# Starting one score tile in seven on ScalarE in layers 1 and 2 of a three-layer graph attention kernel

## The chip, the cores and the metric

The kernel runs on one core of a Trainium2 chip. The metric is the device time in microseconds (us), lower is better. A core has TensorE (PE, matrix products into PSUM), VectorE (DVE), ScalarE (ACT, activations), GpSimd (POOL) and SyncE (SP, here the queue that starts most DMAs). They run side by side, each works through its own instructions in order, and they wait for one another on semaphores.

## The reference

Three graph attention layers over the same 8192 x 8192 adjacency matrix, 64 features a node. Layer 0 is a layer with its own weights, layers 1 and 2 are the two steps of a second block:

```python
# layer 0
scores = (Wh @ a1)[:, None] + (We @ a2)[None, :]
e = jnp.where(scores > 0, scores, ALPHA * scores)      # ALPHA = 0.2
e = jnp.where(adj > 0, e, NEG_BIG)
attention = jax.nn.softmax(e, axis=1)
x = _layernorm(x + elu(attention @ entity_embs + item_embs))
# layers 1 and 2 (i = 0, 1)
Wh = h @ W_l
e = leaky_relu(u + v.T + c)                            # u, v: one number a node
att = softmax(where(adj_mask, e, NEG_INF), axis=1)
h = ALPHA * x + (1.0 - ALPHA) * elu(att @ Wh)
# at the end
x = _layernorm(x + concat(x, h1, h2) @ mlp_w + mlp_b)
```

So each layer needs, for each pair of a row i and a neighbour j, exp of a leaky ReLU of u_i + v_j, masked by the adjacency, then its product with the features of j and the sum over j as denominator.

## The kernel before

**Tiling.** The scores are held transposed: a tile has 128 neighbours j on the partitions and 512 rows i in the free dimension. A layer has 16 blocks of 512 rows (`NB`, index b), a block has 64 tiles (`NT`, index j or t). Tile j of a block is made in four stages on three engines:

1. *The fill* puts the unmasked score into one of five PSUM buffers (`ES = 5`, `eps`). It has two forms. On DVE (`start_scores`, L1044): max(ua + v8, cb), where ua is a row made once a block (u times 0.8 plus cb), v8 one number a partition and cb the row of negated row maxima. On ACT (`start_scores`, L530): Relu(0.8 u + v8) without cb. Both can only begin when the exponential of the tile that had the buffer is done, in general tile j - 5 (`freed`).
2. *The mask product* on PE (`mask_scores`, L680) adds -9e15 where there is no edge. Where the fill was ACT's, a product ahead of it (L677) of a matrix of ones with `mrow`, the row maxima in three bf16 parts, adds cb to all partitions.
3. *The exponential* on ACT (`probs`, L538) goes from PSUM to one of eight buffers in SBUF (`prob`).
4. *The sums* on PE, once in four tiles and one group of four behind (`LAGQ = 1`): features times probabilities (L717, `acc`) and the denominators (L726, `den`).

Which tiles ACT fills is given by `ACT_TILES`, a tuple of residues of j modulo 7 for each layer, and `ON_ACT`, the set made from it for j from 3 on. Before, layer 0 has the residues 2 and 5 (17 tiles a block), layers 1 and 2 none.

**Order of the work.** It is written out by hand: at step t of a block PE does the mask product of tile t and, after every fourth, the sums of the group before; DVE fills tile t; ACT does the exponential of tile t - 1 and, where tile t + 3 (`AHEAD = 3`) is in `ON_ACT`, its fill. The end of block b - 1 (its tail: evacuate, normalise, ELU, next layer's products) and the preparation of block b + 1 (its head) are spread over the steps of block b:

- steps 35 to 43: PE counts edges by level (L690) on bytes that DVE has made (L892, steps 29 to 41); ACT copies the counts out at step 45 (L582), PE turns them at step 47 (L699);
- steps 51, 52 and 53 (`T_HEAD`): DVE does behind its fill of the step nine small instructions on the row maxima (L910 to L923), then two (L930, L931), then three (L934 to L936) that split them in bf16 parts;
- step 56: PE turns the parts (L753), ACT copies them to `mrow` (L586); step 57: PE spreads them (L758), ACT copies them to `cb` (L590); step 63: DVE makes `ua` (L1050).

The last block of a layer has no head. In layer 0 DVE also makes the bit mask from the adjacency as it arrives (L883); layers 1 and 2 read the finished mask back from HBM. At the start of a layer PE also sums the features (L704) between the tiles of block 0.

The lines that use `ON_ACT` outside the counting of semaphores:

```python
# DVE, step t
if t not in ON_ACT[l]:
    start_scores(l, b, t, par)                         # L1044
# ACT, step t, behind the exponential of tile t - 1
if t + AHEAD in ON_ACT[l]:
    start_scores(l, b, t + AHEAD, par)                 # L530
# PE, mask_scores
if on_act:
    nc.tensor.matmul(et, onesb[:, :], mrow[:, par, :], start=False, stop=False, skip_group_check=True)   # L677
```

Of the kernel before, what the change touches and what calls it, by code (L numbers as in the profile page):

```python
# [48 lines left out]
AHEAD = 3  # L49
LAGQ = 1  # L50

ACT_TILES = ((2, 5), (), ())
ON_ACT = tuple(frozenset(j for j in range(AHEAD, NT) if j % 7 in ks) for ks in ACT_TILES)
WC = 2 * C + 2

# [1124 lines left out]
```

## Time and profile before

| | |
|---|---|
| median of 3 runs | 3828.65 us (3826.26 to 3828.78) |
| the profiled execution, its own time | 3827.47 us |
| its span, first to last instruction | 3825.7 us |
| mean granted TensorE clock | 0.983 |
| PE busy (matmuls) | 3542.9 us, 93% |
| DVE busy | 2898.3 us, 76% |
| ACT busy | 2247.2 us, 59% |
| ACT fills (L530) | 272, 189.6 us |
| exponentials (L538) | 3072, 1927.5 us |

In a timeline row the columns are start (us from the span's start), time covered, engine, line, operation, output and inputs by the program's names, shapes and number of instructions, and in brackets the idle time of the engine ahead of it with what ended it. Matmuls are pipelined: each shows its whole passage, which is longer than the pitch at which they follow each other, so the distance between starts tells what one costs. Layer 1 has its first mask product at 1441.84, layer 2 at 2645.20.

### The profile page before, as it was taken

To read this page: it belongs to the slowest core of one execution; us is meant where nothing else is said; L and a number is where in the kernel's file an instruction comes from. 1 tells how busy PE (TensorE), PEld (TensorE's weight loads), DVE (VectorE), ACT (ScalarE), POOL (GpSimd) and SP (SyncE) were. 2 spreads that over 40 slices of the span, in tenths; PEclk is the share of its full clock that TensorE was granted. 3 is DMA by queue.
4 is the path that set the end of the run, shared out by engine and by line. 5 is a ranking of instruction groups with operands and counts; after the bars stand their busy time and mean duration, and the time that the engine had idled before them with its cause. 6 is when DMAs were issued, how large, how long until landed. Compare 5 with 4: busy or idle time off the path is not lost. (4 is left out here: it accounts for less than half of the span.)

```text
span 3825.7 us, 54496 instructions
## 1 busy us (share of the span) xinstructions
PE 3542.9 (93%) x21133; PEld 1136.5 (30%) x21133; DVE 2898.3 (76%) x5279; ACT 2247.2 (59%) x3947; POOL 116.3 (3%) x138
## 2 busy tenths in 40 slices
PE   1689999999999979999999999997999999999998
PEld 0323233323232324332332232323323323323322
DVE  4578888888888656777777777775777877877876
ACT  0356667667766744655655665663556556556555
POOL 0000000000000000000000000000000000000000
PEclk9999999999999988999999999997999999999999
DMA  8999999999999511122121121111111111111110
GB/s 258 292 350 338 327 337 333 336 335 332 337 338 333 170 56 51 53 81 72 59 80 65 67 77 67 67 56 67 60 66 65 72 69 65 67 73 65 64 43 6
DMA packets 414101, 578.47 MB, mean 151 GB/s; under 512 B 294402, under 2 KB 315010, under 8 KB 389266
## 3 DMA queue, kind: packets, MB, share of 16 engines
q1 hardware_dynamic: 409458, 564.40, 45.8%
q0 software_dynamic: 4384, 10.59, 0.9%
q8 instruction: 166, 2.72, 0.3%
q14 instruction: 93, 0.76, 0.1%
HBM read 430.10 MB, written 77.69 MB: 133 GB/s over the span
## 5 line engine op out<-in xcount | busy, mean ns | idle before, releaser
L538 ACT ACTIVATE prob<-eps,v2col 128x512 f32<-128x512 f32 x3072 | 1927.5, 689 | 1125.1 <-PE eps L680 1121.8
L1044 DVE SCALAR_TENSOR_TENSOR eps<-ua,v8col,cb 128x512 f32<-128x512 f32 x2800 | 1990.6, 754 | 619.2 <-ACT prob L538 609.6
L717 PE MATMUL acc<-prob,feat 128*64 128x512 f32 x6144 | 1497.8, 608 | 0.0
L680 PE MATMUL eps<-nt,nbig 128*128 128x512 fp8e4 x3072 | 903.6, 384 | 95.1 <-DVE eps L1044 95.0
L726 PE MATMUL den<-prob,ones 128*32 128x512 f32 x6144 | 820.0, 606 | 0.0
L717 PEld LDWEIGHTS acc<-prob,feat 128*64 128x64 f32 x6144 | 375.2, 136 | 744.8 <-issue 501.9
L680 PEld LDWEIGHTS eps<-nt,nbig 128*128 128x128 bf16 x3072 | 277.9, 101 | 780.9 <-DVE eps L1044 520.3
L883 DVE TENSOR_SCALAR mi<-stage 128x1024 uint8<-128x1024 int32 x512 | 351.8, 689 | 62.1 <-DMA stage<-in_adj_dram 61.9
L726 PEld LDWEIGHTS den<-prob,ones 128*32 128x32 f32 x6144 | 121.0, 108 | 626.6 <-issue 626.6
L892 DVE TENSOR_SCALAR edges<-nt 128x2048 int32<-128x2048 int32 x192 | 234.4, 1221 | 47.3 <-PE misc L690 32.5
L690 PE MATMUL misc<-edges,oneh 128*32 128x512 fp8e4 x3072 | 191.1, 391 | 71.7 <-DVE edges L892 56.9
L530 ACT ACTIVATE eps<-ub,v8col 128x512 f32<-128x512 f32 x272 | 189.6, 697 | 0.0
L690 PEld LDWEIGHTS misc<-edges,oneh 128*32 128x32 bf16 x3072 | 90.3, 99 | 192.2 <-issue 75.6
L586 ACT ACTIVATE mrow<-misc 3x512 bf16<-3x512 bf16 x48 | 28.2, 587 | 141.6 <-PE misc L753 141.6
L677 PE MATMUL eps<-mrow,onesb 128*128 128x512 bf16 x272 | 104.0, 382 | 0.0
L582 ACT ACTIVATE hs<-misc 128x512 f32<-128x512 f32 x48 | 28.3, 590 | 95.2 <-PE misc L690 95.2
L784 PE MATMUL misc<-wcat,ht 65*128 65x130 f32 x384 | 71.6, 311 | 8.6 <-ACT pj L573 6.6
L766 PE MATMUL misc<-halves,acc_s 128*128 128x64 f32 x384 | 75.8, 279 | 2.4 <-ACT hs L547 2.4
L784 PEld LDWEIGHTS misc<-wcat,ht 65*128 65x128 f32 x384 | 52.5, 198 | 69.9 <-issue 37.7
L704 PEld LDWEIGHTS misc<-feat,ones 128*128 128x128 f32 x384 | 65.8, 237 | 13.5 <-issue 10.3
L959 DVE SCALAR_TENSOR_TENSOR g<-fsum,emp,misc 128x65 f32<-128x65 f32 x192 | 41.2, 277 | 36.5 <-PE misc L768 30.2
L910 DVE TENSOR_SCALAR he<-misc 128x128 int32<-128x128 int32 x48 | 14.0, 292 | 70.9 <-PE misc L699 70.9
(140 smaller groups left out, 1251.6 us busy)
## 6 DMA issues: line engine op xcount, KB each, us to landing
stage<-in_adj_dram SPq DMA_DIRECT2D x512, 512.0 KB, 6.3
nt<-nt_d SPq DMA_DIRECT2D x128, 1024.0 KB, 5.0
nt_d<-nt SPq DMA_DIRECT2D x64, 1024.0 KB, 7.1
ub<-u_d SPq DMA_DIRECT2D x48, 256.0 KB, 5.5
xy_d<-xin POOLq DMA_DIRECT2D x32, 256.0 KB, 2.8
xin<-xy_d SPq DMA_DIRECT2D x32, 256.0 KB, 2.9
nt<-mi SPq DMA_TRANSPOSE x256, 6.7
xin<-in_x_dram SPq DMA_DIRECT2D x16, 128.0 KB, 6.1
```

Source lines behind the costliest of these rows:

```text
L530: nc.scalar.activation(eps[:, j % ES, :], ub[:, par, :], ACT.Relu, bias=v8col[:, j:j + 1], scale=1.0 - ALPHA).then_inc(s_filla, 1)
L538: nc.scalar.activation(prob[:, j % TS, :], eps[:, j % ES, :], ACT.Exp, bias=v2col[:, j:j + 1]).then_inc(s_p, 1)
L677: nc.tensor.matmul(et, onesb[:, :], mrow[:, par, :], start=False, stop=False, skip_group_check=True)
L680: nc.tensor.matmul(et, nbig[:, :], half_block(nt[:, par, m, :], m, o), start=False, stop=True, skip_group_check=True).then_inc(s_z, 1)
L690: mm = nc.tensor.matmul(misc[s * HB:(s + 1) * HB, :], oneh[:, m * MT + j, :], half_block(edges[:, n % 2, :], m, j), start=(m == 0 and k == 0),
L717: mm = nc.tensor.matmul(acc[h:h + C, :], feat[:, l % 2, j, 0:C], prob[:, j % TS, :], start=(k == 0), stop=(k == NT // 2 - 1))
L726: mm = nc.tensor.matmul(den[32 * i:32 * i + 32, :], ones[:, 0:32], prob[:, (QUAD * k + i) % TS, :], start=(k == 0), stop=(k == NT // QUAD ...
L766: nc.tensor.matmul(misc[:, r * CE:r * CE + C], acc_s[:, r * P:(r + 1) * P], halves[:, 0:C], start=True, stop=True)
L784: mm = nc.tensor.matmul(misc[:, r * WC:(r + 1) * WC], ht[:, (2 * i + r) * P:(2 * i + r + 1) * P], wcat[:, l, :], start=True, stop=True)
L883: dv.tensor_scalar(out, src, 0, ONE8, ALU.is_le, ALU.mult).then_inc(s_mask, 1)
L892: dv.tensor_scalar(edges[:, n % 2, :].bitcast(I32), nt[:, b % 2, m, :].bitcast(I32), EDGE_FLIP, None, ALU.bitwise_xor).then_inc(s_xor, 1)
L1044: dv.scalar_tensor_tensor(eps[:, j % ES, :], ua[:, par, :], v8col[:, j:j + 1], cb[:, par, :], ALU.add, ALU.max).then_inc(s_fill, 1)
```

## The change

The residue 3 is added for layers 1 and 2. Tiles 3, 10, 17, 24, 31, 38, 45, 52 and 59 of each of their blocks are filled by ACT and no longer by DVE, and PE does the product with `mrow` for them.

```diff
-ACT_TILES = ((2, 5), (), ())
+ACT_TILES = ((2, 5), (3,), (3,))
 ON_ACT = tuple(frozenset(j for j in range(AHEAD, NT) if j % 7 in ks) for ks in ACT_TILES)
```

How that moves instructions, at the head in steps 51 to 54 of a block of layer 1. On DVE before, from the seventh of the nine small instructions on (L1044 a fill, L918 to L923 the row maxima, L930 to L936 the split):

```order
L918 SCALAR_TENSOR_TENSOR ns<-vm,gst,vucol 128x4
L920 SCALAR_TENSOR_TENSOR nm<-ns 128x4
L923 SCALAR_TENSOR_TENSOR nm<-vucol,nm 128x4
L1044 SCALAR_TENSOR_TENSOR eps<-ua,v8col,cb 128x512
L930 CAST parts<-nm 128x4
L931 TENSOR_TENSOR r<-nm,parts 128x4
L1044 SCALAR_TENSOR_TENSOR eps<-ua,v8col,cb 128x512
L934 CAST parts<-r 128x4
L935 TENSOR_TENSOR nm<-r,parts 128x4
L936 CAST parts<-nm 128x4
L1044 SCALAR_TENSOR_TENSOR eps<-ua,v8col,cb 128x512 x10
```

And DVE in the same place now:

```order
L918 SCALAR_TENSOR_TENSOR ns<-vm,gst,vucol 128x4
L920 SCALAR_TENSOR_TENSOR nm<-ns 128x4
L923 SCALAR_TENSOR_TENSOR nm<-vucol,nm 128x4
L930 CAST parts<-nm 128x4
L931 TENSOR_TENSOR r<-nm,parts 128x4
L1044 SCALAR_TENSOR_TENSOR eps<-ua,v8col,cb 128x512
L934 CAST parts<-r 128x4
L935 TENSOR_TENSOR nm<-r,parts 128x4
L936 CAST parts<-nm 128x4
L1044 SCALAR_TENSOR_TENSOR eps<-ua,v8col,cb 128x512 x9
```

The fill between L923 and L930, that of tile 52, is gone from DVE. PE before, from the turned counts (L699) to the turned maxima (L753), tiles 48 to 56:

```order
L699 MATMUL misc<-fold,hs 128x32 x4
L680 MATMUL eps<-nt,nbig 128x512 x4
L717 MATMUL acc<-prob,feat 64x512 x4
L726 MATMUL den<-prob,ones 32x512 x4
L680 MATMUL eps<-nt,nbig 128x512 x4
L717 MATMUL acc<-prob,feat 64x512 x4
L726 MATMUL den<-prob,ones 32x512 x4
L680 MATMUL eps<-nt,nbig 128x512
L753 MATMUL misc<-identb,parts 3x128 x4
```

And PE in the same place now:

```order
L699 MATMUL misc<-fold,hs 128x32 x4
L680 MATMUL eps<-nt,nbig 128x512 x4
L717 MATMUL acc<-prob,feat 64x512 x4
L726 MATMUL den<-prob,ones 32x512 x4
L677 MATMUL eps<-mrow,onesb 128x512
L680 MATMUL eps<-nt,nbig 128x512 x4
L717 MATMUL acc<-prob,feat 64x512 x4
L726 MATMUL den<-prob,ones 32x512 x4
L680 MATMUL eps<-nt,nbig 128x512
L753 MATMUL misc<-identb,parts 3x128 x4
```

The product with `mrow` stands ahead of the mask product of tile 52. On ACT, from the copy of the counts (L582) to that of the maxima (L586), there stood eleven exponentials in a row; now:

```order
L582 ACTIVATE hs<-misc 128x512
L538 ACTIVATE prob<-eps,v2col 128x512 x4
L530 ACTIVATE eps<-ub,v8col 128x512
L538 ACTIVATE prob<-eps,v2col 128x512 x7
L530 ACTIVATE eps<-ub,v8col 128x512
L586 ACTIVATE mrow<-misc 3x512
```

The two L530 are the fills of tiles 52 and 59, behind the exponentials of tiles 48 and 55.

## Rows read from the trace of the kernel before

**Rows 1.** The page: busy times, then two groups (busy, mean ns of one, idle before).
```profile
PE 3542.9 (93%) x21133; PEld 1136.5 (30%) x21133; DVE 2898.3 (76%) x5279; ACT 2247.2 (59%) x3947; POOL 116.3 (3%) x138
...
L1044 DVE SCALAR_TENSOR_TENSOR eps<-ua,v8col,cb 128x512 f32<-128x512 f32 x2800 | 1990.6, 754 | 619.2 <-ACT prob L538 609.6
...
L677 PE MATMUL eps<-mrow,onesb 128*128 128x512 bf16 x272 | 104.0, 382 | 0.0
```

**Rows 2.** Busy time by stretch: layer 1, layer 2 (busy of PE, PEld, DVE, ACT, POOL, clock).
```profile
1485.00:2600.00 1115.00, 1088.26 (x6552) 332.40 (x6545) 854.15 (x1460) 670.66 (x1202) 19.28 (x30) 1.00 0.18 67
2690.00:3780.00 1090.00, 1066.13 (x6435) 326.41 (x6433) 865.02 (x1618) 649.78 (x1107) 42.59 (x30) 1.00 0.17 63
```

**Rows 3.** Timeline of PE, first group of a block of layer 1.
```profile
2178.19 1.04 PE L680 MATMUL eps<-nt,nbig 128*128 128x512 fp8e4 x4
...
2181.02 1.07 PE L726 MATMUL den<-prob,ones 128*32 128x512 f32 x8
2182.02 1.04 PE L680 MATMUL eps<-nt,nbig 128*128 128x512 fp8e4 x4
```

**Rows 4.** Waits in layer 1, 1480 to 2640 (total us, times, longest).
```profile
ACT prob L538 <- PE eps L680: 355.5, 234, 3.4
...
PE eps L680 <- DVE eps L1044: 18.8, 45, 0.7
```

**Rows 5.** Waits of PE in layer 2, 2690 to 3790.
```profile
PE eps L680 <- DVE eps L1044: 18.5, 45, 0.7
```

**Rows 6.** Timeline of PE, the same block, tiles 52 to 55.
```profile
2163.76 0.39 PE L680 MATMUL eps<-nt,nbig 128*128 128x512 fp8e4 x1
2164.37 0.39 PE L680 MATMUL eps<-nt,nbig 128*128 128x512 fp8e4 x1 [0.23 <-DVE eps L1044]
2165.51 0.39 PE L680 MATMUL eps<-nt,nbig 128*128 128x512 fp8e4 x1 [0.75 <-DVE eps L1044]
2166.17 0.39 PE L680 MATMUL eps<-nt,nbig 128*128 128x512 fp8e4 x1 [0.27 <-DVE eps L1044]
```

**Rows 7.** Timeline of DVE in the same place, steps 51 to 54.
```profile
2160.14 0.29 DVE L910 TENSOR_SCALAR he<-misc 128x128 int32<-128x128 int32 x1 [1.25 <-PE misc L699]
...
2162.29 0.16 DVE L923 SCALAR_TENSOR_TENSOR nm<-vucol,nm 128x4 f32<-128x4 f32 x1
2162.49 0.76 DVE L1044 SCALAR_TENSOR_TENSOR eps<-ua,v8col,cb 128x512 f32<-128x512 f32 x1
...
2163.55 0.76 DVE L1044 SCALAR_TENSOR_TENSOR eps<-ua,v8col,cb 128x512 f32<-128x512 f32 x1
...
2164.70 2.74 DVE L1044 SCALAR_TENSOR_TENSOR eps<-ua,v8col,cb 128x512 f32<-128x512 f32 x4
```

**Rows 8.** Timeline of PE in layer 0, an ACT-filled tile.
```profile
748.68 0.38 PE L677 MATMUL eps<-mrow,onesb 128*128 128x512 bf16 x1
748.90 0.81 PE L680 MATMUL eps<-nt,nbig 128*128 128x512 fp8e4 x3
```

**Rows 9.** Busy time by stretch, start of layer 2 (columns of rows 2).
```profile
2645.00:2653.00 8.00, 7.79 (x35) 7.33 (x36) 5.64 (x9) 3.44 (x5) 0.00 (x0) 0.50 0.00 1
```

**Rows 10.** Timeline of ACT: tiles 48 to 51, step 56, tiles 60 to 63.
```profile
2160.41 2.42 ACT L538 ACTIVATE prob<-eps,v2col 128x512 f32<-128x512 f32 x4 [1.82 <-PE eps L680]
...
2170.09 0.59 ACT L586 ACTIVATE mrow<-misc 3x512 bf16<-3x512 bf16 x1 [2.81 <-PE misc L753]
...
2174.84 2.42 ACT L538 ACTIVATE prob<-eps,v2col 128x512 f32<-128x512 f32 x4 [1.34 <-PE eps L680]
```

**Rows 11.** Timelines of DVE (fills from tile 42) and PE (masks 40 to 43).
```profile
2148.80 4.78 DVE L1044 SCALAR_TENSOR_TENSOR eps<-ua,v8col,cb 128x512 f32<-128x512 f32 x7
...
2149.62 1.05 PE L680 MATMUL eps<-nt,nbig 128*128 128x512 fp8e4 x4
```

**Rows 12.** Groups of ACT in layer 0, 400 to 1200.
```profile
L530 ACT ACTIVATE eps<-ub,v8col 128x512 f32<-128x512 f32 x176 | 122.7, 697 | 0.0
```

**Rows 13.** Timeline of PE, start of the block that ends at rows 3.
```profile
2105.91 1.04 PE L680 MATMUL eps<-nt,nbig 128*128 128x512 fp8e4 x4
```

## The prediction

> **What bounds the kernel now.** I read the busy table first [rows 1]. The reader is to see TensorE (PE) at 93% of the span, VectorE (DVE) at 76% and ScalarE (ACT) at 59%. The change touches layers 1 and 2 alone, so the next view is the busy time by stretch [rows 2]. In 1,115 us of layer 1 PE is busy for 1,088.26, in 1,090 us of layer 2 for 1,066.13, with the granted clock at 1.00. Idle PE is some 27 and 24 us, idle DVE 261 and 225 us. A busy PE need not be at its peak, so I looked at how its instructions follow each other. In a plain group of four tiles [rows 3] the mask products start at 2178.19 and those of the next group at 2182.02: 3.83 us a group, and no row carries an idle time. PE issues its work in one unbroken line, and the other two engines fit beside it.
>
> Where does it wait? PE's waits in layer 1 [rows 4] have one entry that counts: mask products (L680) that wait for a DVE fill (L1044), 18.8 us in 45 times. Layer 2 has 18.5 us in 45 [rows 5]. 45 is three a block for the 15 blocks with a successor. The timeline of PE shows the place [rows 6]: tiles 52 to 55 start at 2163.76, 2164.37, 2165.51 and 2166.17. Four products whose fills are ready span 1.04 us, of which the last shows 0.38, so their pitch is (1.04 - 0.38)/3 = 0.22; I use 0.217. The gaps 0.61, 1.14 and 0.66 less 0.217 each leave 0.39 + 0.92 + 0.44 = 1.76 us of stall a block. (The waits list gives only 18.8/15 = 1.25, since the 0.38 us that a product shows reach past its pitch and cover part of each gap.)
>
> The timeline of DVE says why [rows 7]. At step 51 DVE waits until 2160.14 for the turned counts (PE L699), then does nine small steps on the row maxima (the last at 2162.29), and only then fill 52 (2162.49), two small steps, fill 53 (2163.55), three small steps and fill 54 (2164.70). Four fills in a row take 2.74 us and one 0.76, so their pitch is (2.74 - 0.76)/3 = 0.66 us.
>
> **The change part by part.** The tiles with j % 7 = 3 are 3, 10, 17, 24, 31, 38, 45, 52, 59: nine a block, 9 x 16 x 2 = 288 in layers 1 and 2. Layer 0 keeps its own.
>
> *Added on PE: 288 products of 128x512 (L677).* Layer 0 does the same thing and has the rows [rows 8]: L677 starts at 748.68 and the mask product behind it at 748.90, 0.22 us later, with no wait for the changed weights. I take 0.217: 288 x 0.217 = 62.5 us. The high end is 0.23 (66 us). The low end is what a denominator product costs, 8 in the 1.00 us from 2181.02 to 2182.02 [rows 3], 0.125 (36 us); those run side by side in parts of the array, which a product of 128 rows by 128 columns cannot, so I stay with the row of the thing itself. In the first microseconds of a layer the granted clock is 0.50, the lower level of 1.2 GHz [rows 9], and the pitch double. Only tile 3 of block 0 falls there: 0.2 us more a layer, 0.4 in all. Added: 62.9 us. Since PE runs without a gap nearly everywhere, all of it is on the path.
>
> The Trainium skill has a rule that speaks for a smaller price: "TensorE: Matmul & The Clock Gate", section "Back-to-back issue gap", puts pairs of weight load and 512-column product in a stream at about 131 ns each, and a single gap at about 216. By the first the added products would cost an estimated 288 x 0.131 = 37.7 us, by the second 62.2. The rows are such a stream and show 0.22: the trace sides with the second.
>
> *Removed from DVE: 288 fills* of 754 ns [rows 1], 0.66 us of pitch each. Nearly all of that frees an engine that had time. It counts only at tiles 53 to 55. Tile 52 is one of the nine, so no fill remains between the ninth small step and the first of the split. Everything behind it on DVE moves up by 0.66: fill 53 ends at 2163.65 instead of 2164.31, fill 54 at 2164.79, fill 55 at 2165.45. On PE the extra product takes 2163.76, mask 52 goes at 2163.98, mask 53 at 2164.19 (its fill is there), mask 54 waits until about 2164.85 and mask 55 until about 2165.51 (a fill's end plus the 0.06 between fill 53 and mask 53 today). Mask 55 starts 0.66 us earlier than before although the group has a product more: the stall falls from 1.76 to 1.76 - 0.66 - 0.22 = 0.88 us. Recovered: 0.88 x 15 blocks x 2 layers = 26.4 us. The bounds are 0 (something else holds tiles 53 to 55) and all 1.76 (52.8 us).
>
> *Added on ACT: 288 fills (L530)* of 697 ns [rows 12], 200 us in all, on an engine that in layer 1 waits 355.5 us for mask products [rows 4]. A group's four exponentials take 2.42 us of 3.83 and ACT waits 1.34 between groups [rows 10], so a fill of 0.69 fits. What it can hurt is the in-order queue: fill j stands behind the exponential of tile j - 4. Tile 3 is the tightest: exp 63 ends at 2174.84 + 2.42 = 2177.26 [rows 10], the fill near 2177.95, and mask 3 starts 0.65 after 2178.19 [rows 3]: 0.8 us in hand. For tile 52, exp 48 (2160.41 + 0.69) puts the fill's end near 2161.8, 2 us before it is wanted. Tile 59's fill goes ahead of the copy that waits 2.81 us for the turned maxima [rows 10]. Behind each ACT fill up to three exponentials slip by 0.6 us, and DVE fills wait for them, since buffer j is free once exp j - 5 is done. That matters where DVE has nothing in hand, at tile 43: its fill ends at 2148.80 + 0.66 + 0.76 = 2150.22 and its mask product starts at 2149.62 + 1.05 - 0.38 = 2150.29 [rows 11]. But that chain starts at exp 36, fill 38 goes before exp 35, and the added product in group 36 to 39 gives DVE 0.22 more. I price ACT at nothing; the cover is its wait between groups. If that were gone in one group a block, a late fill would cost at most its 0.69: 32 x 0.69 = 22 us.
>
> *Other queues.* SP and POOL issue nothing new and are not moved past.
>
> **Sum.** +62.9 - 26.4 = +36.5 us on the profiled execution. A block with a successor gets 9 x 0.217 - 0.88 = 1.07 us longer (2178.19 - 2105.91 = 72.28 [rows 3, 13] becomes 73.35), the last of a layer 1.95. The profiled execution took 3827.47 us (span 3825.7), within the three runs shown and 1.2 below their median of 3828.65. So 3827.47 + 36.5 = 3864.0, or 3865.2 against the median. I forecast 3864.5, 0.94% slower.
>
> **The rivals.**
> 1. *ACT fills come late.* PE waits for ACT once a block instead. For it: the fills meet ACT's copies at steps 4, 5, 25 and 45. Against: in layer 0 ACT does 176 fills in 800 us [rows 12], more than the nine per 72 us here, and finds room. At 0.3 us a block (half of the 0.6 by which an exponential slips) 32 x 0.3 = 10: 3874. Chance 0.07.
> 2. *Nothing is recovered*, because exponentials or counts hold tiles 53 to 55. Against: the four exponentials from 48 on are done at 2162.83 [rows 10], and with a fill among them at 2163.4, before they are wanted. 3827.5 + 62.9 = 3890. Chance 0.04.
> 3. *The stall goes altogether.* For it, the small steps may close up with no fill between. Against: fills 54 and 55 keep their pitch, and three small steps stay. 3827.5 + 62.9 - 52.8 = 3838. Chance 0.04.
> 4. *The product costs 0.125*, as one beside its neighbours would: 3827.5 + 36 - 26.4 = 3837. Chance 0.02. Against: rows 8.
> 5. *Faster: DVE is the true bound.* At tiles 52 to 55 the stall vanishes (52.8), and the added product overlaps its neighbours. It decides from a price under 52.8/288 = 0.183 us a product; at 0.125 it gives 3827.5 + 36 - 52.8 = 3811. Against: rows 8, and 261 us of idle DVE. Chance 0.01.
>
> The Trainium skill stands behind the idea of rival 5: "Perfetto Trace Analysis", section "Optimizing Scalar/DVE Operations", says that where DVE is saturated, moving work to Scalar may make sense. The 261 us of idle DVE in layer 1 show that the condition is not met, and the rule does not count the product that PE gets with it.
>
> **How the numbers follow.** The forecast has 0.82, the rivals 0.07, 0.04, 0.04, 0.02 and 0.01. Its own spread is a few us (products at 0.21 to 0.23, recovery 20 to 30): 3856 to 3874. The range goes to 3855 and, past rival 1, to 3878, and leaves out the other four, 0.11. A measurement of this kernel tells about 0.2% (7.7 us) from no change. All cases but rival 5 are above that, rivals 3 and 4 barely (10 us), so half of their 0.06 counts as same: faster 0.02, same 0.03, slower 0.95.
>
> **What would show it.** L677 goes from 272 to 560 products, L530 from 272 to 560, L1044 from 2,800 to 2,512. Steady blocks of layer 1 last 73.35 us, and no block of layer 0 changes. PE's waits for L1044 fall from three to two a block, tiles 54 and 55, and no entry names L530. DVE's busy time falls by 217 us and ACT's rises by 200 while the time gets longer. The forecast is wrong if blocks of layer 1 grow by 1.95 (rival 2) or by 0.2 (rivals 3 and 4), if PE waits for L530 (rival 1), or if a product's pitch in layer 1 is not 0.22.

## The result and the profile after

| | before | after |
|---|---|---|
| median | 3827.45 us (3824.72 to 3828.78, 4 runs) | 3865.59 us (3861.55 to 3868.34, 4 runs) |
| ratio of the runs | | 1.0095 (95% interval 1.0083 to 1.0107) |
| span of the profiled execution | 3825.7 us | 3863.6 us |

The change makes the kernel 1.0% slower: 38.1 us between the medians, and the interval of the ratio holds it. The forecast was 3864.5 us, 0.94% slower. DVE has less to do, ACT more, and the time went to PE. The page of the changed kernel (busy times; then groups with busy time, mean ns of one, idle before):

```profile
PE 3572.6 (92%) x21147; PEld 1162.8 (30%) x21421; DVE 2731.1 (71%) x4991; ACT 2414.2 (62%) x4235; POOL 117.0 (3%) x138
...
L530 ACT ACTIVATE eps<-ub,v8col 128x512 f32<-128x512 f32 x560 | 389.5, 696 | 1.0
...
L677 PE MATMUL eps<-mrow,onesb 128*128 128x512 bf16 x319 | 122.2, 383 | 0.0
...
L677 PEld LDWEIGHTS eps<-mrow,onesb 128*128 128x128 bf16 x560 | 56.8, 101 | 117.6 <-issue 99.4
```

Against [rows 1] DVE has 288 instructions fewer; ACT has its 288 fills more. DVE's busy time fell by 167.2 us and ACT's rose by 167.0, where 217 and 200 had been forecast: busy time counts the stretch in which two rows overlap once (four fills cover 2.74 us [rows 7], not 4 x 0.754), and the forecast took every row at its full length. The time of the kernel doesn't hang on this. The products are 560, as the weight loads show; of the matmul rows only 319 are in the trace. Where a record is missing, the two matmuls beside it start some 0.43 us apart in place of 0.22, and a wait may be put down to the wrong line, so the lengths below are taken between rows that are both there.

PE's waits in layer 1 after (total us, times, longest), which answer to [rows 4]:

```profile
PE eps L680 <- ACT mrow L586: 8.7, 15, 0.6
PE eps L680 <- DVE eps L1044: 8.0, 30, 0.3
```

Waits for fills fell from 18.8 us in 45 to 8.0 in 30, three a block to two. No entry names L530, the fills of ACT. The first row isn't new: the waits of before have it as L758, the product that spreads the maxima, for the same `mrow`, 5.4 us in 15. Where the record of L758 is missing its wait is put on the next line.

The timeline of PE after at the head, tiles 48 to 55, answers to [rows 6]:

```profile
2172.53 1.03 PE L680 MATMUL eps<-nt,nbig 128*128 128x512 fp8e4 x4
...
2176.36 0.39 PE L677 MATMUL eps<-mrow,onesb 128*128 128x512 bf16 x1
2176.58 0.59 PE L680 MATMUL eps<-nt,nbig 128*128 128x512 fp8e4 x2
2177.43 0.39 PE L680 MATMUL eps<-nt,nbig 128*128 128x512 fp8e4 x1 [0.26 <-DVE eps L1044]
2178.10 0.39 PE L680 MATMUL eps<-nt,nbig 128*128 128x512 fp8e4 x1 [0.27 <-DVE eps L1044]
2178.42 1.94 PE L717 MATMUL acc<-prob,feat 128*64 128x512 f32 x8
```

The added product stands at 2176.36, masks 52 and 53 follow it at once, and 54 and 55 still wait, by the distances between starts some 0.88 us together (1.76 before). From mask 48 to the sums behind tile 55 it is 2178.42 - 2172.53 = 5.89 us. The same two rows of before:

```profile
2159.93 1.03 PE L680 MATMUL eps<-nt,nbig 128*128 128x512 fp8e4 x4
...
2166.49 1.94 PE L717 MATMUL acc<-prob,feat 128*64 128x512 f32 x8
```

That was 6.56 us. So this stretch is 0.67 us shorter, with one product more in it. At the other eight tiles the product is an addition, as the length of a block shows. The starts of two blocks after answer to [rows 3, 13]:

```profile
2117.00 0.82 PE L680 MATMUL eps<-nt,nbig 128*128 128x512 fp8e4 x3
2117.66 0.38 PE L677 MATMUL eps<-mrow,onesb 128*128 128x512 bf16 x1
2117.87 0.38 PE L680 MATMUL eps<-nt,nbig 128*128 128x512 fp8e4 x1
...
2190.33 0.82 PE L680 MATMUL eps<-nt,nbig 128*128 128x512 fp8e4 x3
```

A block takes 73.33 us, where it took 72.28 (73.35 was forecast). Between L677 and L680 lie 0.21 us.

DVE after, in the same place, answers to [rows 7]:

```profile
2174.88 0.16 DVE L923 SCALAR_TENSOR_TENSOR nm<-vucol,nm 128x4 f32<-128x4 f32 x1
...
2175.48 0.76 DVE L1044 SCALAR_TENSOR_TENSOR eps<-ua,v8col,cb 128x512 f32<-128x512 f32 x1
```

From L923 to fill 53 it is 0.60 us, where it was 2163.55 - 2162.29 = 1.26: one fill's pitch less.

### The profile page after: what moved, and what is told of

It is laid out like the page before. It is cut to its first block and busy times, and to the rows that moved or that the text cites. A ratio compares the mean times of both kernels' runs of the same rounds, so it can differ in the third digit from the quotient of the medians.

```text
span 3863.6 us, 54830 instructions
## 1 busy us (share of the span) xinstructions
PE 3572.6 (92%) x21147; PEld 1162.8 (30%) x21421; DVE 2731.1 (71%) x4991; ACT 2414.2 (62%) x4235; POOL 117.0 (3%) x138
## 5 line engine op out<-in xcount | busy, mean ns | idle before, releaser
L1044 DVE SCALAR_TENSOR_TENSOR eps<-ua,v8col,cb 128x512 f32<-128x512 f32 x2512 | 1818.5, 756 | 818.1 <-ACT prob L538 806.9
L717 PE MATMUL acc<-prob,feat 128*64 128x512 f32 x6144 | 1499.1, 609 | 0.0
L680 PE MATMUL eps<-nt,nbig 128*128 128x512 fp8e4 x3072 | 932.8, 384 | 115.5 <-DVE eps L1044 78.2
L726 PE MATMUL den<-prob,ones 128*32 128x512 f32 x6144 | 819.5, 605 | 0.0
L717 PEld LDWEIGHTS acc<-prob,feat 128*64 128x64 f32 x6144 | 375.2, 136 | 750.9 <-issue 482.3
L680 PEld LDWEIGHTS eps<-nt,nbig 128*128 128x128 bf16 x3072 | 285.1, 101 | 714.4 <-DVE eps L1044 457.7
L530 ACT ACTIVATE eps<-ub,v8col 128x512 f32<-128x512 f32 x560 | 389.5, 696 | 1.0
L726 PEld LDWEIGHTS den<-prob,ones 128*32 128x32 f32 x6144 | 121.0, 108 | 628.2 <-issue 628.2
L677 PE MATMUL eps<-mrow,onesb 128*128 128x512 bf16 x319 | 122.2, 383 | 0.0
L586 ACT ACTIVATE mrow<-misc 3x512 bf16<-3x512 bf16 x48 | 28.1, 586 | 116.4 <-PE misc L753 116.4
L677 PEld LDWEIGHTS eps<-mrow,onesb 128*128 128x128 bf16 x560 | 56.8, 101 | 117.6 <-issue 99.4
L582 ACT ACTIVATE hs<-misc 128x512 f32<-128x512 f32 x48 | 28.2, 588 | 95.8 <-PE misc L690 95.8
```

The source lines that it names most:

```text
L530: nc.scalar.activation(eps[:, j % ES, :], ub[:, par, :], ACT.Relu, bias=v8col[:, j:j + 1], scale=1.0 - ALPHA).then_inc(s_filla, 1)
L680: nc.tensor.matmul(et, nbig[:, :], half_block(nt[:, par, m, :], m, o), start=False, stop=True, skip_group_check=True).then_inc(s_z, 1)
L717: mm = nc.tensor.matmul(acc[h:h + C, :], feat[:, l % 2, j, 0:C], prob[:, j % TS, :], start=(k == 0), stop=(k == NT // 2 - 1))
L726: mm = nc.tensor.matmul(den[32 * i:32 * i + 32, :], ones[:, 0:32], prob[:, (QUAD * k + i) % TS, :], start=(k == 0), stop=(k == NT // QUAD ...
L1044: dv.scalar_tensor_tensor(eps[:, j % ES, :], ua[:, par, :], v8col[:, j:j + 1], cb[:, par, :], ALU.add, ALU.max).then_inc(s_fill, 1)
```

## The experiments

Each is compared with runs of the kernel before on the same chip. The medians of before were 3829.55 us (9 runs) beside the first four and 3827.83 (7 runs) beside the last two, so medians of different sets can differ by some 2 us with nothing changed. In the kernels whose file is two lines longer, L682 stands for L680, L679 for L677, L1046 for L1044, L719 for L717.

**Tile 52 alone.** What is the one useful tile of the nine worth? The diff is against the changed kernel.

```diff
-ACT_TILES = ((2, 5), (3,), (3,))
-ON_ACT = tuple(frozenset(j for j in range(AHEAD, NT) if j % 7 in ks) for ks in ACT_TILES)
+ACT_TILES = ((2, 5), (), ())
+MORE = ((), (52,), (52,))
+ON_ACT = tuple(frozenset(j for j in range(AHEAD, NT) if j % 7 in ks or j in more)
+               for ks, more in zip(ACT_TILES, MORE))
```

> Of the nine tiles only tile 52 is filled by ACT in layers 1 and 2. Theory (a product costs its pitch of 0.217 us on PE wherever fills are ready; DVE sets the end of group 52 to 55): in a block with a head the product is absorbed and DVE's chain is one fill pitch, 0.66 us, shorter, so 30 x -0.66 + 2 x 0.22 = -19.5 us against before: 3808, faster than both kernels. PE waits for L1044 at tiles 54 and 55, some 0.44 each. Rival A (the stall shrinks since DVE as a whole has less to do, so all nine tiles share in it): little is recovered and 32 products are added, 3827 to 3834. Rival B (the cost of the change lies in the ACT fills, not in the products): like the theory's sign, but less than 19 us.

Measured: 3808.43 us (3806.28 to 3812.97), ratio 0.9948 (0.9934 to 0.9962). The theory gave 3808. Rivals A and B fall: 21 us were won, by one tile. The timeline of PE in layer 1, from tile 48 to the sums behind tile 55:

```profile
2153.85 1.03 PE L682 MATMUL eps<-nt,nbig 128*128 128x512 fp8e4 x4
...
2157.90 0.59 PE L682 MATMUL eps<-nt,nbig 128*128 128x512 fp8e4 x2 [0.16 <-issue]
2158.76 0.39 PE L682 MATMUL eps<-nt,nbig 128*128 128x512 fp8e4 x1 [0.27 <-DVE eps L1046]
2159.43 0.39 PE L682 MATMUL eps<-nt,nbig 128*128 128x512 fp8e4 x1 [0.27 <-DVE eps L1046]
2159.74 0.65 PE L719 MATMUL acc<-prob,feat 128*64 128x512 f32 x2
```

2159.74 - 2153.85 = 5.89 us, exactly as with all nine tiles. (The 0.16 by "issue" is the product, whose record is missing.) The other eight tiles gave nothing back there.

**Tiles 52 and 54.** The same edit with two tiles, to see whether the mechanism goes on. The diff is against the kernel with tile 52 alone.

```diff
-MORE = ((), (52,), (52,))
+MORE = ((), (52, 54), (52, 54))
```

> Tiles 52 and 54 are filled by ACT in layers 1 and 2, no other. Theory: DVE has only fills 53 and 55 left in the group, fill 55 is ready 1.33 us earlier than in the kernel before, at 0.06 before mask 55 could go anyway; group 52 to 55 ends 1.32 us earlier although it has two products more. 30 x -1.32 + 4 x 0.22 = -38.7 us: 3789, 1.0% faster than before, and PE's waits for L1044 in layers 1 and 2 nearly gone. Rival A: 3834 to 3841. Rival C (exponentials slipped by two ACT fills hold tile 55): like e1, 3808.

Measured: 3789.54 us (3788.76 to 3790.28), ratio 0.9895 (0.9882 to 0.9909); expected 3789. The same stretch:

```profile
2148.56 1.03 PE L682 MATMUL eps<-nt,nbig 128*128 128x512 fp8e4 x4
...
2152.61 0.59 PE L682 MATMUL eps<-nt,nbig 128*128 128x512 fp8e4 x2 [0.16 <-issue]
2153.04 0.38 PE L679 MATMUL eps<-mrow,onesb 128*128 128x512 bf16 x1
2153.26 0.61 PE L682 MATMUL eps<-nt,nbig 128*128 128x512 fp8e4 x2
2153.80 0.65 PE L719 MATMUL acc<-prob,feat 128*64 128x512 f32 x2
```

5.24 us, no wait for DVE is left, and the list of PE's waits in layer 1 has no row for L1046 any more. Two fills off the chain are 1.32 us, and the two products are covered. Rival C, exponentials that hold tile 55, falls.

**Residue 2 in place of 3.** Tiles 9, 16, ..., 51, 58: eight a block, none of them on DVE between the row maxima and tile 55. The diff is against the changed kernel.

```diff
-ACT_TILES = ((2, 5), (3,), (3,))
+ACT_TILES = ((2, 5), (2,), (2,))
```

> Residue 2 in place of 3 in layers 1 and 2: tiles 9, 16, 23, 30, 37, 44, 51, 58, eight a block, none between the row maxima and tile 55. Theory: nothing is taken from DVE's chain at the head, since fill 51 ends before DVE waits for the counts; the product ahead of mask 51 falls into the time that PE would lose at tiles 53 to 55. 30 x 7 x 0.217 + 2 x 8 x 0.217 = +49 us: 3876, slower than the change although it adds 32 products fewer; stall at 53 to 55 about 1.54 us a block. Rival A (less work on DVE anywhere helps): 8/9 of the change, 3861.

Measured: 3877.01 us (3876.06 to 3878.76), ratio 1.0124 (1.0110 to 1.0138); expected 3876. With fewer products than the change it is 11 us slower, and rival A (3861) falls once more. PE's waits in layer 1, then the timeline at the head:

```profile
PE eps L680 <- DVE eps L1044: 15.3, 30, 0.7
```

```profile
2177.26 0.81 PE L680 MATMUL eps<-nt,nbig 128*128 128x512 fp8e4 x3
2177.90 0.38 PE L677 MATMUL eps<-mrow,onesb 128*128 128x512 bf16 x1
...
2183.81 1.94 PE L717 MATMUL acc<-prob,feat 128*64 128x512 f32 x8
```

2183.81 - 2177.26 = 6.55 us: the stretch has its old length, since the chain of DVE does, and the product at tile 51 lies inside it.

**The change without its product.** The row term is left out of the scores of the nine tiles of layers 1 and 2; ACT's fills stay. The diff is against the changed kernel.

```diff
-                if on_act:
+                if on_act and l == 0:
```

> The changed kernel without its row-term product in layers 1 and 2 (that part of the scores is left out for nine tiles in 64; layer 0 as it was). Theory: 288 products go. In 30 blocks the one at tile 52 was free, so 30 x 8 x 0.217 + 2 x 9 x 0.217 + 0.4 = 56.4 us less than the change, and what is left against before is DVE's shorter chain, 30 x -0.66: 3808. Rival B (ACT fills or their handshake cost): stays well above 3827. Rival D (a product costs 0.125, the rest of the 38 us is something else): 3865 - 33 = 3832.

Measured: 3809.56 us (3807.52 to 3812.26), ratio 0.9948 (0.9934 to 0.9962); expected 3808. The 288 products alone make the difference between this and the change: 56.0 us between the two medians, 58.1 when each is taken against its own runs of before (+38.1 and -20.0). Divided by 288 that is 0.19 to 0.20 us each; by the 258 that the theory counts as exposed it is 0.217 to 0.225. Without their products the 288 fills on ACT give the time of tile 52 alone (3808.43), so the other 256 cost nothing that these runs can tell. Rivals B and D fall. PE at the head, from mask 48 on:

```profile
2082.20 1.03 PE L680 MATMUL eps<-nt,nbig 128*128 128x512 fp8e4 x4
...
2087.12 0.39 PE L680 MATMUL eps<-nt,nbig 128*128 128x512 fp8e4 x1 [0.48 <-DVE eps L1044]
...
2088.10 1.08 PE L717 MATMUL acc<-prob,feat 128*64 128x512 f32 x4
```

5.90 us, as with the product. It only waits 0.48 at tile 54 instead of 0.26. The product at tile 52 costs nothing.

**The product alone.** All fills of layers 1 and 2 stay on DVE, and a product with zero weights is added at the nine tiles. The diff is against the kernel before and leaves out three edits: `ZERO` (for layers 1 and 2 the tiles with j % 7 = 3), the memory for `zerob` with its filling, and the count that DVE waits for because of it.

```diff
-                if on_act:
+                if on_act or j in ZERO[l]:
-                    nc.tensor.matmul(et, onesb[:, :], mrow[:, par, :], start=False, stop=False,
+                    nc.tensor.matmul(et, onesb[:, :] if on_act else zerob[:, :], mrow[:, par, :], start=False, stop=False,
```

> The kernel before (all fills of layers 1 and 2 on DVE) with one more product of the same shape ahead of the mask product of the tiles 3, 10, ..., 59 of layers 1 and 2; its weights are zeros, so the result stays. Theory: in a block with a head eight of the nine cost their 0.217 us and the one at tile 52 falls into the time that PE loses to DVE at tiles 53 to 55; the last block of a layer pays nine. 30 x 8 x 0.217 + 2 x 9 x 0.217 + 0.4 = +56.4 us: 3884, slower than the change itself by 18 to 19 us, which is what the fill taken from DVE at tile 52 was worth. Rival B (the cost of the change is in its ACT fills): 3828 to 3840. Rival E (all nine cost, and the recovery was 26.4 as the prediction had it by another way): 3890.

Measured: 3885.28 us (3882.62 to 3888.85), ratio 1.0149 (1.0132 to 1.0166), 57.5 us over before; expected 56.4. Between this and the change lie the 288 fills taken from DVE, 19.7 us by the medians; tile 52 alone, which won 21, says that it is the fill at tile 52. Rival B falls. Rival E (3890: all nine products cost) is only 5 us away in time, but the trace excludes it: the stretch from mask 48 to the sums behind tile 55 would be 0.22 us longer than before, and it is 6.55 us again; the product at tile 52 only replaces waiting:

```profile
2180.00 1.03 PE L682 MATMUL eps<-nt,nbig 128*128 128x512 fp8e4 x4
...
2183.82 0.39 PE L679 MATMUL eps<-mrow,zerob 128*128 128x512 bf16 x1
...
2185.57 0.39 PE L682 MATMUL eps<-nt,nbig 128*128 128x512 fp8e4 x1 [0.75 <-DVE eps L1046]
...
2186.55 1.94 PE L719 MATMUL acc<-prob,feat 128*64 128x512 f32 x8
```

**Layer 0 by the same rule.** A version that is faster still. The diff is against the kernel with tiles 52 and 54; in layer 0 ACT has 13 fills a block in place of 17.

```diff
-ACT_TILES = ((2, 5), (), ())
-MORE = ((), (52, 54), (52, 54))
+ACT_TILES = ((), (), ())
+MORE = ((3, 9, 12, 16, 19, 22, 26, 30, 33, 40, 52, 54, 61), (52, 54), (52, 54))
```

> As the kernel with tiles 52 and 54 in layers 1 and 2; in layer 0 ACT fills 13 tiles and not 17: 3, 9, 12, 16, 19, 22, 26, 30, 33, 40, 52, 54, 61. The rule is the same: ACT where PE stands waiting for DVE (3, 22, 52, 54), the product saved where DVE has time in hand (37, 44, 47, 58). Theory: in blocks 1 to 14 of layer 0 0.55 at tile 3, 0.43 at tile 22, 0.66 at 52 to 55 and 4 x 0.217, some 2.5 us a block less, and up to 3 us lost in block 0 where DVE makes more mask units: 3789.5 - 32 = 3757. Rival F (layer 0 is bound by DVE and its mask making, so fills given back to it cost 0.66 each): 16 x 4 x 0.66 = 42 us more: 3832.

Measured: 3763.74 us (3761.93 to 3764.65), ratio 0.9830 (0.9816 to 0.9845). Rival F falls, but the time is 7 us over the 3757 expected. PE in a block of layer 0 in this kernel:

```profile
775.49 1.25 PE L682 MATMUL eps<-nt,nbig 128*128 128x512 fp8e4 x4
...
799.03 0.39 PE L682 MATMUL eps<-nt,nbig 128*128 128x512 fp8e4 x1 [0.48 <-DVE eps L1046]
...
823.14 0.39 PE L682 MATMUL eps<-nt,nbig 128*128 128x512 fp8e4 x1 [0.22 <-DVE eps L1046]
...
838.91 0.39 PE L682 MATMUL eps<-nt,nbig 128*128 128x512 fp8e4 x1 [0.92 <-DVE eps L1046]
...
851.14 0.82 PE L682 MATMUL eps<-nt,nbig 128*128 128x512 fp8e4 x3
```

The block takes 75.65 us. Before it was 788.63 - 711.26 = 77.37:

```profile
711.26 0.82 PE L680 MATMUL eps<-nt,nbig 128*128 128x512 fp8e4 x3
712.50 0.39 PE L680 MATMUL eps<-nt,nbig 128*128 128x512 fp8e4 x1 [0.41 <-DVE eps L1044]
734.79 0.39 PE L680 MATMUL eps<-nt,nbig 128*128 128x512 fp8e4 x1 [0.32 <-DVE eps L1044]
...
774.44 0.39 PE L680 MATMUL eps<-nt,nbig 128*128 128x512 fp8e4 x1 [0.60 <-DVE eps L1044]
776.18 0.39 PE L680 MATMUL eps<-nt,nbig 128*128 128x512 fp8e4 x1 [0.92 <-DVE eps L1044]
788.63 0.82 PE L680 MATMUL eps<-nt,nbig 128*128 128x512 fp8e4 x3
```

1.72 us a block were won, not 2.5; 0.87 of them are the four products saved. The waits at tiles 3 and 53 are gone. The one at tile 22 moved to tile 23 (0.48), whose fill I had given back to DVE behind the same work, a small one at tile 43 grew, and the one at tile 55 stayed at 0.92, since mask making stands in DVE's queue there (a row of 0.69 us at 837.50, right ahead of the fill at 838.10).

## Why the prediction was right

The times of whole runs scatter by a few us: the first mask product of layer 1 comes at 1441.84 before, at 1442.39 after and at 1444.78 with the product alone, though layer 0 is the same in all three. The lengths of steady blocks hardly do, so the sharpest test of each term is the distance between the first mask products of two blocks in the middle of layer 1:

| kernel | first masks of the two blocks | block, us | by the theory |
|---|---|---|---|
| before | 2105.91, 2178.19 | 72.28 | |
| the change | 2117.00, 2190.33 | 73.33 | 72.28 + 8 x 0.217 - 0.66 = 73.36 |
| tile 52 alone | 2099.82, 2171.44 | 71.62 | 72.28 - 0.66 = 71.62 |
| tiles 52 and 54 | 2094.54, 2165.50 | 70.96 | 72.28 - 1.32 = 70.96 |
| residue 2 | 2121.94, 2195.72 | 73.78 | 72.28 + 7 x 0.217 = 73.80 |
| without the product | 2099.80, 2171.41 | 71.61 | 72.28 - 0.66 = 71.62 |
| the product alone | 2124.47, 2198.47 | 74.00 | 72.28 + 8 x 0.217 = 74.02 |

*The price of the added product.* It held to about a per cent. A block of the change is 1.72 us longer than one of the kernel without the product, 0.215 for each of eight; the product alone adds as much to the kernel before. In whole times the first difference is 56.0 to 58.1 us, by the prediction's terms 56.4 (62.9 less the 30 at tile 52 of 0.217 each, which cost nothing). That PE has no room at the other eight tiles is shown by the product alone: 57.5 us. The figure of 131 ns a product that the prediction cited from the Trainium skill ("TensorE: Matmul & The Clock Gate", "Back-to-back issue gap") doesn't hold for these pairs; the rows show 0.21 to 0.23 at a granted clock of 1.00, near the 216 ns that the same section gives for a single gap.

*The recovery.* 0.88 us a block were forecast from moving DVE's chain up by one fill. The stretch from mask 48 to the sums behind tile 55 became 0.67 us shorter with a 0.217 product inside, together 0.89. Shown from both sides: tile 52 alone brings the stretch to the same 5.89 us as all nine, residue 2, without it, leaves it at 6.55, and a second fill off the same chain brings the same again.

*ACT at nothing.* No wait of PE for L530 is in the trace of the change. With ACT's 288 fills but without the products the kernel is 20 us faster than before, and a block has the length that tile 52 alone gives it, 71.61 against 71.62.

*The rivals.* Late ACT fills, no recovery, full recovery, a cheaper product and DVE as the bound each asked for a block length that wasn't there. The nearest to being tempting, that DVE is the bound, was excluded by its own condition: a product costs 0.217 where it had to be under 0.183. Eight fills a block taken from DVE at other tiles than 52 leave the block as long as it was (71.61 against 71.62).

*The sum.* +36.5 was forecast, +37.9 is what the spans show. Part of so close a hit is luck, given the scatter of whole runs. Of the missing 1.4 us, 0.55 are there before layer 1 begins (1442.39 in place of 1441.84), where the change does nothing. From there to the first mask of layer 2 (2664.90 after) layer 1 took 19.15 us more, where 15 x 1.07 + 1.95 + 0.2 = 18.2 were forecast; layer 2 took the forecast 18.2 more. The 0.9 in layer 1 is about the size of what the clock cost at its start, shown next. Busy time by stretch at the start of layer 1 (busy of PE, PEld, DVE, ACT, POOL; granted clock, DMA share, GB/s), before and after:

```profile
1456.00:1461.00 5.00, 5.00 (x42) 3.43 (x40) 1.61 (x3) 2.06 (x3) 0.00 (x0) 1.00 0.00 0
```

```profile
1456.00:1461.00 5.00, 5.00 (x28) 2.09 (x25) 0.14 (x1) 0.48 (x1) 0.00 (x0) 0.74 0.00 0
```

After, the lower level (0.50, 1.2 GHz) ended at about 1456 + (1 - 0.74)/0.5 x 5 = 1458.6, 16.2 us behind the first mask product; before it ended at about 1455.5, 13.7 us behind it (the granted clock is 0.74 from 1455 to 1456). PE had worked without a pause from the first mask product on in both. The first sums of the layer (L717 and L726, eight rows each) fall there: from 1453.58 to 1457.39 before, 3.81 us, and from 1454.56 to 1459.33 after, 4.77. With the product alone, where PE has the same order of work, the lower level ended 13.8 us behind the first mask product (1444.78; the granted clock is 0.61 from 1457.78 to 1458.78), so the added products alone don't bring this. What does stays open.

## What to carry to other kernels

A busy share of 93% and an idle list of 50 us say little; the distance between the starts of consecutive matmuls says whether PE has a gap, and a product added where it has none costs its full pitch (here 0.217 us for 512 columns at a granted clock of 1.00). When work is moved to relieve an engine, ask for each piece whether the bound engine waits there: here one tile of the nine paid (-21 us) and the other eight cost 57 to 59, and placed by the waits rather than by a residue the same idea gave 1.0% in two layers and, with four products a block saved in layer 0, 1.7% in three. Added work was free inside a wait that another engine ends: at tile 52 the stretch is 5.89 us with the product and 5.90 without it, at tile 51 it kept its length (6.55, and 6.56 before). To judge one term of a sum, compare the lengths of steady blocks: here they agreed with the theory to 0.03 us, where whole runs of the changed kernel lie up to 6.8 us apart.

## What had not been expected

- In one execution of the changed kernel the granted clock came back 2.5 us later behind the start of layer 1 than before, which cost about 1 us.
- The trace of the changed kernel lacks 241 of 560 rows for one matmul while the weight loads are all there. Records of L758 are missing in the same way. Their waits appear on the next line, as above.
